# Mixture of low-rank maps in a two-block transformer kernel: middle products made already turned, weights spread by a selection matrix and applied after the first product, final stores in pairs of tiles

## The reference, cut to what matters

```python
x = L0_attn_X                                  # (2, 1024, 256), 16 heads of 16
x = _layernorm(x + attention(layernorm(x)))    # causal, softmax
# mixture, K = 8 experts of rank R = 64:
h = relu(einsum('bsd,de->bse', x, W1) + b1)
alpha = softmax(einsum('bse,ek->bsk', h, W2) + b2, axis=-1)
vx = einsum('krd,bsd->bskr', V, x)
uvx = einsum('kdr,bskr->bskd', U, vx)
x = _layernorm(x + einsum('bsk,bskd->bsd', alpha, uvx))
```

## Time and profile before

| | |
|---|---|
| median of 3 runs | 431.72 us (431.71, 431.72, 434.21) |
| the profiled execution | 431.88 us, its span 429.9 us |
| PE busy | 405.0 us, 94% of the span |
| DVE busy | 307.0 us, 71% |
| ACT busy | 243.3 us, 57% |
| POOL busy | 78.5 us, 18% |
| chain that ended last | PE 76%, DVE 15%, ACT 6%, DMA 1% |
| mean granted TensorE clock | 0.996 |

### The profile page before, as it was taken

One profiled execution on the slowest core, in us unless ns is written; L12 is line 12 of the kernel. 1 busy time (PEld: TensorE's weight loads), 2 busy tenths in 40 slices (PEclk: granted clock), 3 DMA queues, 4 the chain that ended last, 5 costly groups with the idle time before them and its releaser, 6 DMA issues.

```text
span 429.9 us, 7414 instructions
## 1 busy us (share of the span) xinstructions
PE 405.0 (94%) x2565; PEld 213.7 (50%) x2565; DVE 307.0 (71%) x807; ACT 243.3 (57%) x541; POOL 78.5 (18%) x115
## 2 busy tenths in 40 slices
PE   7997899999999989999999999999999998999994
PEld 3545444344334444476668734344334444446783
DVE  5548997798798676438488799789889863213665
ACT  6646555666777576443451264667676847642421
POOL 4422211143250110102240022113212011020000
PEclk9999999999999999999999999999999999999998
DMA  6167860450402000002673045054130000000011
GB/s 196 23 97 101 196 97 10 74 76 8 72 19 82 2 2 0 2 1 74 106 130 59 26 79 91 7 84 70 20 57 3 0 3 1 2 0 2 0 50 49
DMA packets 18452, 21.14 MB, mean 49 GB/s; under 512 B 4976, under 2 KB 11888, under 8 KB 18416
## 3 DMA queue, kind: packets, MB, share of 16 engines
q1 hardware_dynamic: 18365, 20.66, 25.7%
q10 hardware_dynamic: 51, 0.01, 0.0%
HBM read 5.79 MB, written 2.10 MB: 18 GB/s over the span
## 4 chain that ended last, share of the span: by engine, by line
PE 76%; DVE 15%; ACT 6%; issue 2%; DMA 1%; POOL 0%; ACTq 0%; DVEq 0%; POOLq 0%
PE ps L953 19%; PE ps L1068 14%; PE ps L1047 14%; PE ps L1024 10%; DVE mx L824 8%; PE ps L961 8%; PE ps L969 4%; PE ps L944 2%; ACT pr L683 2%; PE ps L1028 2%; PE ps L1142 2%; PE ps L1078 1%; DVE ps L820 1%; ACT stk L604 1%; DMA stq<-mrow 1%
## 5 line engine op out<-in xcount | busy, mean ns | idle before, releaser
L683 ACT ACTIVATE pr<-ps 128x512 f32<-128x512 f32 (+3 forms) x384 | 165.9, 495 | 95.3 <-PE ps L1047 93.8
L824 DVE TENSOR_REDUCE mx<-ps 128x1 f32<-128x512 f32 (+3 forms) x240 | 145.7, 665 | 14.6 <-PE ps L1024 7.4
L1047 PE MATMUL ps<-stq,stk 99*128 99x512 bf16 (+3 forms) x384 | 116.2, 330 | 4.8 <-ACT pr L683 3.3
L1024 PE MATMUL ps<-stk,stq 96*128 96x512 bf16 (+3 forms) x384 | 112.5, 327 | 1.4 <-DVE mx L824 0.6
L595 POOL TENSOR_SCALAR_AFFINE_SELECT pr<-pr 128x512 f32<-128x512 f32 x64 | 40.9, 639 | 245.9 <-ACT pr L683 245.9
L1068 PE MATMUL ps<-pr,va 128*32 128x512 f32 (+3 forms) x768 | 81.8, 498 | 0.0
L1047 PEld LDWEIGHTS ps<-stq,stk 99*128 99x128 bf16 x384 | 34.4, 98 | 90.8 <-ACT pr L683 51.8
L1024 PEld LDWEIGHTS ps<-stk,stq 96*128 96x128 bf16 x384 | 37.5, 98 | 21.4 <-issue 5.6
L820 DVE CUSTOM_DVE_ANT_0 ps<-ps,causal 128x384 f32<-128x384 f32 (+1 forms) x64 | 38.5, 648 | 11.6 <-PE ps L1024 11.6
L1028 PE MATMUL ps<-mask,ident_b 128*128 128x128 bf16 x192 | 35.2, 219 | 0.0
L953 PE MATMUL ps<-u_t,avt 128*128 128x256 f32 x128 | 30.8, 383 | 0.3 <-ACT avt L719 0.2
(11 more groups left out here) (108 smaller groups left out, 389.1 us busy)
## 6 DMA issues: line engine op xcount, KB each, us to landing
stq<-qk_raw SPq DMA_DIRECT2D x32, 96.0 KB, 2.8
stk<-qk_raw SPq DMA_DIRECT2D x32, 96.0 KB, 2.8
x_in<-in_x SPq DMA_DIRECT2D x8, 256.0 KB, 3.5
stq<-qk_raw SPq DMA_DIRECT2D x32, 64.0 KB, 2.4
stk<-qk_raw SPq DMA_DIRECT2D x32, 64.0 KB, 2.4
out_y<-x SPq DMA_DIRECT2D x3, 512.0 KB, 3.1
stk<-qk_raw SPq DMA_DIRECT2D x32, 32.0 KB, 2.4
stq<-qk_raw SPq DMA_DIRECT2D x32, 32.0 KB, 2.1
```

Source lines behind the costliest of these rows:

```text
L683: nc.scalar.activation(probs(b, g, s)[:, j, q0 - c * CHUNK:], act_bank(ev)[:, q0 - c * CHUNK:], ACT.Exp, scale=DH ** -0.5).then_inc(s_act_ ...
L824: nc.vector.tensor_reduce(dst, src, AX.X, ALU.max).then_inc(s_dve_free, 1)
L1024: last = nc.tensor.matmul(bank[:, i * w:(i + 1) * w], q[0:ROWS, t // TPC, j, tile(t % TPC)], k[0:ROWS, k0 // CHUNK, j, 0:w], start=True, s ...
L1047: nc.tensor.matmul(bank[:, q0 - c * CHUNK:], stk[stack_of(b, g)][0:ROWS + PARTS, kt // TPC, j, tile(kt % TPC)], stq[stack_of(b, g)][0:ROWS ...
```

## The change

The first product's operands change sides: `vx` is now an event for one of RC = 4 ranks r (128 of the 512 middle columns) and all four tiles of the chunk, so it leaves the middle space down the partitions and the rows across, which is what the second product needs. The transposes `avt` go. The weights must then run the same way: DVE splits alpha into three bfloat16 parts (four small operations, `alpha_parts`), `arow` turns them in one product and ACT copies them (`alpha_rows`, 96x128), `ex` spreads them with four bfloat16 products per rank against `selection`, a matrix of zeros and ones, and ACT copies the result to `spread` (two buffers). DVE then multiplies product and spread into `avt` (four ranks kept). `u` of any tile needs all four ranks. POOL makes `choice`, and ACT widens it once to `selection`. At the very end tiles 4 and 5 share one loop over the ranks (`with_last`), and the last four tiles are normalised and stored as two pairs where there were two single tiles and a pair. The row bv no longer goes into `flat`.

```diff
-        ts = chunk_tiles(c)
-        o = [[("vx", b, t)] * (t in ts) + [("avt", b, t - 1)] * (t - 1 in ts) + [("u", b, t - 2)] * (t - 2 in ts)
-             for t in range(ts[0], ts[-1] + 3)]
-        return [e for part in o for e in part]
+        ex, vx = ([(kind, b, c, r) for r in range(ranks)] for kind in ("ex", "vx"))
+        return [("arow", b, c)], ex, vx, [("u", b, t) for t in chunk_tiles(c)]
...
-        m = [maps(b, c) for c in range(C)]
+        arow, ex, vx, u = zip(*[maps(b, c) for c in range(C)])
         beside = {35: res[0][:parts], 36: res[0][parts:parts + 1], 37: res[0][parts + 1:-1], 38: res[0][-1:], 40: mix[0][0],
-                  41: mix[0][1][:parts], 42: mix[0][1][parts:], 43: [("alpha", b, 0)] + m[0][:1], 44: m[0][1:2],
-                  45: m[0][2:4], 46: m[0][4:5] + m[0][6:7], 47: m[0][5:6], 48: m[0][7:8]}
+                  41: mix[0][1][:parts], 42: mix[0][1][parts:], 43: [("alpha", b, 0)] + vx[0][:1], 44: vx[0][1:2] + arow[0],
+                  45: ex[0][:1] + vx[0][2:3] + ex[0][1:2], 46: vx[0][3:], 47: ex[0][2:], 48: u[0][:1]}
...
-            before = m[1]
+            before = arow[1] + [ev for pair in zip(ex[1], vx[1]) for ev in pair] + u[1]
             qk, (here, xt, later) = first[parts:-1], (first[-1:], second[:parts], [("stack", nb, 1, 0)])
-            order += qk[:1] + ot + m[0][8:10] + [r4, r6, n] + qk[1:2] + m[0][10:11] + qk[2:3] + [("load", nb)] + turned
-            order += qk[3:] + here + later + xt + mixed[:-2] + m[0][11:] + mixed[-2:] + third[b][:1] + [("alpha", b, 1)]
+            order += qk[:1] + ot + u[0][1:2] + [r4, r6, n] + qk[1:2] + u[0][2:3] + qk[2:3] + [("load", nb)] + turned
+            order += qk[3:] + here + later + xt + mixed[:-2] + u[0][3:] + mixed[-2:] + [("alpha", b, 1)] + third[b][:1]
-            h, (lg, weigh), vx = mixed[:parts], mixed[parts:], m[1][:2]
-            order += turn2 + ot + [r4, r6] + norm + [("second", *ev) for ev in norm] + m[0][8:11] + x1t + m[0][11:] + [("stat", b, t) for t in chunk_tiles(0)]
-            order += h + [lg, weigh, ("alpha", b, 1)] + vx + third[b][:1]
-            order += m[1][2:7] + [("ln3", b, TPC, 1)] + m[1][7:9] + [("ln3", b, TPC + 1, 1)]
-            order += m[1][9:] + [("ln3", b, TPC + 2, 2), ("second", "ln3", b, TPC + 2, 2)]
+            h, weighing = mixed[:parts], mixed[parts:] + [("alpha", b, 1)]
+            order += turn2 + ot + [r4, r6] + norm + [("second", *ev) for ev in norm] + u[0][1:3] + x1t + u[0][3:] + [("stat", b, t) for t in chunk_tiles(0)]
+            order += h + weighing + third[b][:1] + vx[1][:2] + arow[1] + vx[1][2:3] + ex[1][:2] + vx[1][3:] + ex[1][2:]
+            stores = [[store, ("second", *store)] for store in (("ln3", b, TPC + 2 * p, 2) for p in range(2))]
+            order += u[1][:3] + stores[0] + u[1][3:] + stores[1]
...
-        avx = sb("avx", [P, 2, ER])
-        avt = sb("avt", [P, 2, ER])
+        alpha_res = sb("alpha_res", [P, TPC, E])
+        alpha_parts = sb("alpha_parts", [P, PARTS, TPC, E], BF16)
+        alpha_rows = sb("alpha_rows", [PARTS * TPC * E, P], BF16)
+        choice = sb("choice", [PARTS * TPC * E, TPC * E], BF16)
+        selection = sb("selection", [PARTS * TPC * E, TPC * E, ER // E], BF16)
+        spread = sb("spread", [P, 2, CHUNK])
+        avt = sb("avt", [P, RC, CHUNK])
...
+        with_last = {("u", NB - 1, TPC + 1)}
...
+            pool.memset(choice[:], 0.0).then_inc(s_choice, 1)
+            for a in range(PARTS):
+                pool.wait_ge(s_choice, a + 1)
+                pool.affine_select(out=choice[:], in_=choice[:], compare_op=ALU.not_equal, fill=1.0, base=-a * TPC * E,
+                                   pattern=[[-1, TPC * E]], channel_multiplier=1).then_inc(s_choice, 1)
...
+                if ev == ("rows", 0, 0, 0):
+                    act.wait_ge(s_choice, PARTS + 1)
+                    nc.scalar.activation(selection[:], choice[:].unsqueeze(2).to_broadcast([PARTS * TPC * E, TPC * E, ER // E]),
+                                         ACT.Copy).then_inc(s_selection, 1)
...
-                if kind == "avt":
-                    t = ev[2]
+                if kind == "arow":
                     act.wait_ge(s_act_full, n_act[ev])
-                    if t >= 2:
-                        act.wait_ge(s_dve_full, n_dve["u", b, t - 2])
-                    nc.scalar.activation(avt[:, t % 2, :], act_bank(ev), ACT.Copy).then_inc(s_act_free, 1)
+                    nc.scalar.activation(alpha_rows[:], act_bank(ev)[0:PARTS * TPC * E, 0:P], ACT.Copy).then_inc(s_act_free, 1)
+                if kind == "ex":
+                    n = n_spread[ev]
+                    act.wait_ge(s_act_full, n_act[ev])
+                    if n > 2:
+                        act.wait_ge(s_dve_free, n_dve["vx", *spreads[n - 3][1:]])
+                    nc.scalar.activation(spread[:, n % 2, :], act_bank(ev), ACT.Copy).then_inc(s_act_free, 1)
...
+                    if n_alpha[ev] > 1:
+                        dve.wait_ge(s_act_full, n_act["arow", *divmod(b * C + c - 1, C)])
+                    link(nc.vector.tensor_copy(alpha_parts[:, 0], alpha[:, c]))
+                    link(nc.vector.tensor_tensor(alpha_res[:], alpha[:, c], alpha_parts[:, 0], ALU.subtract))
+                    link(nc.vector.tensor_copy(alpha_parts[:, 1], alpha_res[:]))
+                    nc.vector.tensor_tensor(alpha_parts[:, 2], alpha_res[:], alpha_parts[:, 1], ALU.subtract).then_inc(s_alpha, 1)
                 if kind == "vx":
-                    t = ev[2]
+                    r = ev[3]
+                    one = "ex", *ev[1:]
                     dve.wait_ge(s_dve_full, n_dve[ev])
-                    if t >= 2:
-                        dve.wait_ge(s_act_full, n_act["avt", b, t - 2])
-                    nc.vector.tensor_tensor(
-                        avx[:, t % 2, :].rearrange("p (e r) -> p e r", e=E),
-                        dve_bank(ev).rearrange("p (e r) -> p e r", e=E),
-                        alpha[:, t // TPC, t % TPC, :].unsqueeze(2).to_broadcast([P, E, ER // E]),
-                        ALU.mult).then_inc(s_dve_free, 1)
+                    dve.wait_ge(s_act_free, n_act[one])
+                    nc.vector.tensor_tensor(avt[:, r, :], dve_bank(ev), spread[:, n_spread[one] % 2, :], ALU.mult).then_inc(s_dve_free, 1)
                 if kind == "u":
                     t = ev[2]
                     dve.wait_ge(s_dve_full, n_dve[ev])
                                        lambda k: w_2[:, k, :], KC)
                     last.then_inc(s_dve_full, 1)
                 if kind == "vx":
-                    t = ev[2]
+                    r = ev[3]
                     bank = take_dve(ev)
                     if b == 0:
                         pe.wait_ge(s_weight_far, n_far["far", 0, "vt", KC - 1])
-                    part_products(bank, lambda i, k: x1_t[:, i, k, tile(t % TPC)], lambda j, k: v_t[:, j, k, :],
+                    part_products(bank, lambda i, k: v_t[:, i, k, tile(r)], lambda j, k: x1_t[:, j, k, :],
                                   ((0, 0), (0, 1), (1, 0)), KC, start=True, stop=True).then_inc(s_dve_full, 1)
-                if kind == "avt":
+                if kind == "arow":
+                    pe.wait_ge(s_alpha, n_alpha["alpha", *ev[1:]])
+                    nc.tensor.matmul(take_act(ev)[0:PARTS * TPC * E, 0:P], alpha_parts[:].rearrange("p a t e -> p (a t e)"),
+                                     ident_b[:], start=True, stop=True).then_inc(s_act_full, 1)
+                if kind == "ex":
+                    _, _, c, r = ev
+                    bank = take_act(ev)
+                    per = P * E // ER
+                    if b == 0:
+                        pe.wait_ge(s_selection, 1)
+                    pe.wait_ge(s_act_free, n_act["arow", b, c])
+                    for t in range(TPC):
+                        mine = selection[:, t * E + r * per:t * E + (r + 1) * per, :]
+                        last = nc.tensor.matmul(bank[:, tile(t)], mine.rearrange("p e r -> p (e r)"),
+                                                alpha_rows[:], start=True, stop=True)
+                    last.then_inc(s_act_full, 1)
+                if kind == "u" and ev not in with_last:
                     t = ev[2]
-                    bank = take_act(ev)
-                    pe.wait_ge(s_dve_free, n_dve["vx", b, t])
+                    both = [ev] + [second for second in with_last if second == ("u", b, t + 1)]
+                    banks = [take_dve(one) for one in both]
+                    weights("ut", b)
                     for r in range(RC):
-                        last = nc.tensor.transpose(bank[:, tile(r)], avx[:, t % 2, tile(r)], ident[:])
-                    last.then_inc(s_act_full, 1)
-                if kind == "u":
-                    t = ev[2]
-                    bank = take_dve(ev)
-                    weights("ut", b)
-                    pe.wait_ge(s_act_free, n_act["avt", b, t])
```

(6 more changed lines are left out.)

32 lines of the change are left out of this document (20 added, 12 removed).

## The result

| | before | after |
|---|---|---|
| median | 431.77 us | 434.75 us |
| the profiled execution | 431.88, span 429.9 | 433.70, span 431.8 |
| PE busy | 405.0 | 403.2 |
| DVE busy | 307.0 | 309.4 |
| ACT busy | 243.3 | 246.2 |

(16 runs each.) The ratio, which leaves out the one run of 2179.96 us (the median is 434.52 without it), is 1.0063, 95% interval 1.0051 to 1.0075: some 2.7 us slower, by less than 1%. The forecast was 433.0, with 429.6 to 435.6 as its range. PE's busy time went down by 1.8 us and the time went up. The scatter grew as well: the 15 runs that lie together span 1.0 us before and 4.9 after.

A forecast was written before the change was run, and what follows sets the result against it. The prediction took PE, with 76% of the chain of waits, as the main bound. Its terms, -1.4 + 2.6 - 1.1 - 0.3 = -0.2, plus 1.4 for the clock, gave +1.2 and a median of 433.0 us, range 429.6 to 435.6.

The forecast's parts named there:

- The stall at (0,1): At (0,1), PE waits 3.35 us at the first spread for ACT's alpha_rows copy; +2.6 with the work saved.
- The fall of the clock: Behind the wait at (0,1), the granted clock drops to 1.2 GHz, costing 1.4 us, bounds 0 and 2.1.
- rival (a): At (0,1), PE's wait is there but the clock stays up: 431.7 us; chance 0.3.
- Work on PE: Every chunk: transposes go, spreading products and one turning product come; -0.70 us a chunk, -2.8 if nothing waits.
- rival (d): At the spreads, each costs 0.22 in place of 0.06 us, +10 in all; chance 0.05 together with (c).
- Rival (c): At u, waits before each rank hold up weight loads: 9.1 us, or 441; chance 0.05 together with (d).
- (0,0) and (1,0): Sums of the terms for the maps at these two places: -1.4 us at (0,0), -1.1 at (1,0).
- the two waits for an exponential: At (0,0) and (1,0), split score products fill PE's waits of 0.61 and 0.29 us: -0.9 each place.
- +0.4 for the first u: At (0,0), the first u needs all four multiplications, three of them behind batch 1's normalisation on DVE: +0.4 us.
- (1,1): At the kernel's end, DVE becomes the bound and its last addition waits for its own queue: -0.3 us.
- The sum: Whole kernel: -0.2 us without the clock, +1.4 for the clock, so +1.2 on the profiled execution's 431.88.

The follow-up runs named there:

- dummies: Changed kernel plus 14 dummy products on TensorE in its wait at (0,1), ahead of the first spread; median 432.55 us, ratio 1.0026 to the kernel before.
- rows_early: Changed kernel with the turning of the weights at (0,1), and so ScalarE's copy, ahead of the first middle part; median 430.92 us, ratio 0.9980 to the kernel before.
- again: The changed kernel, unedited, run once more beside the other experiments; median 435.33 us, ratio 1.0082 to the kernel before.

## Why the prediction was right, point by point

**The stall at (0,1).** Forecast 3.35 us, ended by ScalarE's copy; measured 3.30, and the chain of queues is the one forecast, with each start 1.3 to 1.5 earlier, since the kernel came to this place earlier. (The recorded addition 218.7 + 0.6 + 0.6 + 0.6 is 220.5, not 220.4; the wait by it would be 3.45.) dummies and rows_early show it by experiment: filled, it still costs 2.61 (forecast +2.6); with the copy ahead of the middle parts it is gone but for 1.27.

**The fall of the clock.** Forecast with 1.4 from bounds 0 and 2.1; measured 1.55 and 1.77 by two profiles against dummies'. That it came so near has luck in it. The price was read from the first dummies of the kernel, 15 in 5.39 us, but the granted clock of before reads 1.00 from 0 to 10 us, so no run shows that these were slow by the low level; what fits is the low stretch itself, 3.4 us at half clock. And the row at the kernel's end, from which the fall was expected, does not say when it comes: in before the clock went down 2 to 3 us behind the last product, in after some 5 us. So the doubt in rival (a) was fair, and after's run of 432.29, with a mean clock of 0.998, is probably an execution without the fall. Whole runs show a higher price: again's 435.33 less dummies' 432.55 is 2.8. At most 0.44 of that is the second fall at 42 us in again's profile. The rest, and why that second fall seems rarer in dummies, stays open. The Trainium skill, "TensorE: Matmul & The Clock Gate", section "Why this matters for your kernels", warns of idle gaps between bursts; this trace agrees (3.30 us idle, then 0.50).

**Work on PE.** Forecast -0.70 a chunk. The spreads run as forecast: the chain charges 0.22 to 0.23 for four where it charged 0.44 for four transposes, so 58 ns for one at 0.23, which also ends rival (d). At (0,1) 2.61 of cost less 3.30 of wait gives -0.69. The same page of the Trainium skill, section "Back-to-back issue gap", has 81 ns for such a pair in a sustained stream; the spreads here, in runs of four to eight, take less, so the measurement decides. Rival (c) fell with u at 1.73 to 1.78 a tile on the chain, at every tile that waits for nothing.

**(0,0) and (1,0), where a term was wrong.** Forecast -1.4 and -1.1, measured -0.82 and -0.77. The failed term is "the two waits for an exponential ... should be filled: -0.9". The groups by line of the stretch from logits to logits (163.6 to 209.8 before, 163.2 to 208.5 after), before and then after:

```profile
L1047 PE MATMUL ps<-stq,stk 99*128 99x512 bf16 (+3 forms) x22 | 5.7, 327 | 0.7 <-ACT pr L683 0.6
```

```profile
L1075 PE MATMUL ps<-stq,stk 99*128 99x512 bf16 (+3 forms) x22 | 5.7, 327 | 0.7 <-ACT pr L706 0.7
...
L1178 PE MATMUL ps<-alpha_rows,selection 96*128 96x128 bf16 x16 | 1.6, 219 | 0.3 <-ACT spread L745 0.3
```

The idle time ahead of score products is 0.7 in both. The waits moved and were not filled. The change divides the scores of steps 44 and 47, where before had its two waits on the chain, but at step 46 all four now stand in a row, where avt stood between them before. The chain of after has its waits at steps 45, 46 and 47 (0.50, 0.39 and 0.34): ScalarE has to make as many exponentials in the time. A new 0.3 came for the bank of the last spread. The term measured 0 to +0.3, not -0.9. With 0 in its place the forecast's other terms leave -0.5 at (0,0), and -0.8 with the error of u that follows, which is what was measured. At (1,0) they leave -0.26 where -0.77 was measured: 0.3 of the rest lies behind the layer norm, where no term looked for it (from the end of ScalarE's av_raw to the logits the chain took 17.21 before and 16.89 after), and 0.2 stays open.

The other term there, +0.4 for the first u behind batch 1's normalisation, was also too big. VectorE at (0,0):

```profile
175.11 0.69 DVE L937 TENSOR_TENSOR avt<-ps,spread 128x512 f32<-128x512 f32 x1 [7.09 <-ACT spread L745]
175.72 1.39 DVE L786 BATCH_NORM_STATS2 st<-qk_raw 128x6 f32<-128x256 f32 x4
...
181.69 1.28 DVE L937 TENSOR_TENSOR avt<-ps,spread 128x512 f32<-128x512 f32 x2
```

It idles 7.09 and then runs into the normalisation, as forecast to within 0.3 us; but u took only 0.1 more for it (1.92 on the chain, 1.83 in before). The forecast let u start with all four multiplications; in the kernel it waits rank by rank, it began at 182.75, and the fourth multiplication, from 183.16 to 183.85, was done by the time its last rank was due. The two errors are of opposite sign, 0.9 and 0.3 at (0,0).

**(1,1).** Forecast -0.3 with VectorE as the bound, measured -0.22:

```profile
421.43 0.42 DVE L941 TENSOR_TENSOR x<-ps,x 128x256 f32<-128x256 f32 x1 [1.49 <-PE ps L1189]
...
426.03 0.42 DVE L941 TENSOR_TENSOR x<-ps,x 128x256 f32<-128x256 f32 x1
```

No idle time stands ahead of the last addition, while the earlier trace rows had 0.59 for PE.

**The sum.** Forecast +1.2 on the profiled execution, measured +1.8. The parts: (0,0) +0.6 and (1,0) +0.35 above the forecast, (0,1) +0.15 and (1,1) +0.1 above it, and -0.45 from the start, which is the DMA and no merit of the forecast. That the median lies above the profiled run (434.52, without the one far run, against 433.70), a profile alone could not tell: it holds one of several outcomes of the clock. The mean granted clock of after's runs goes with their times, 0.998 at 432.29, 0.995 at 433.70, 0.988 to 0.989 from 435.17 to 436.49, 0.984 at 437.19. So the forecast of the median was right within its range, but of the 2.7 to 3.0 us that the medians lie apart it foresaw 1.3.

## What to carry to other kernels

A weight that is needed only on the multiplying engine may come late; once it is an operand of the matrix engine, every queue between its making and that product is on the path, and its place in each must be chosen, not only the place of the product. Work out the wait from the queues, row by row, before believing a count of instructions: here one event in another place was worth 3.4 us by the marks and 4.4 by the medians (rows_early against again), and the arithmetic of all four chunks was forecast to save 2.8. And where single runs fall into groups, look for short waits of TensorE, above all ahead of products of few columns: filling two of them with dummies cost nothing that the runs show, and no run lay in the upper groups then (six runs with both filled).
